# A place for the wait on a batch's rows, and an order of their own for the last two batches, in the attention layers of a graph network

## The reference, cut to what matters

```python
def _gat_layer(h, W, al, ar, src, dst, residual):
    feat = (h @ W).reshape(N, 4, 64)
    el, er = jnp.sum(feat * al[None], -1), jnp.sum(feat * ar[None], -1)
    e = leaky_relu(el[src] + er[dst], 0.2)
    ex = jnp.exp(e - segment_max(e, dst)[dst])
    a = ex / segment_sum(ex, dst)[dst]
    out = segment_sum(a[:, :, None] * feat[src], dst)
    return relu(out + h if residual else out)   # the last of the three has no residual
```

## Time and profile before

| | |
|---|---|
| median of three runs | 9299.58 us |
| the profiled execution, own time | 9322.28 us |
| its span | 9320.3 us |
| mean granted TensorE clock | 0.713 |
| the three attention layers | 3505 to 4936, 4937 to 6370, 6371 to about 7800 us |
| batches in a layer | 52 |

### The profile page before, as it was taken

How to read it: one execution, slowest core, us unless ns; L and a number is a source line. 1 busy time by engine, 2 the same in 40 slices (tenths; PEclk the granted TensorE clock), 3 DMA queues, 4 the chain that set the end, 5 groups by cost and what they waited for, 6 DMA issues and landing times. The chain is left out here.

```text
span 9320.3 us, 119336 instructions
## 1 busy us (share of the span) xinstructions
PE 4964.3 (53%) x16882; PEld 3061.1 (33%) x16882; DVE 4504.5 (48%) x11795; ACT 2930.1 (31%) x11603; POOL 4540.5 (49%) x4821
## 2 busy tenths in 40 slices
PE   9755555634444363566664655554656555444444
PEld 4333333423223242333332333332333332222222
DVE  4133333423333264666665666665666665333334
ACT  3200000000000034666663666663666663000000
POOL 0235555445545425555555555554555554554443
PEclk9866676767666686777776777776777777666667
DMA  6422222222222214333333343333333332222221
GB/s 194 141 66 81 82 80 82 73 67 78 72 67 73 64 59 131 107 108 106 107 106 87 106 109 104 107 111 107 109 107 108 105 107 72 77 77 73 77 74 58
DMA packets 449022, 866.69 MB, mean 93 GB/s; under 512 B 123533, under 2 KB 275494, under 8 KB 448266
## 3 DMA queue, kind: packets, MB, share of 16 engines
q0 software_dynamic: 227728, 627.56, 24.3%
q1 hardware_dynamic: 169632, 190.18, 6.3%
q10 hardware_dynamic: 50906, 41.33, 1.4%
HBM read 756.54 MB, written 102.11 MB: 92 GB/s over the span
## 5 line engine op out<-in xcount | busy, mean ns | idle before, releaser
L675 POOL DMA_INDIRECT rows_a<-table,rows_src x2460 | 2338.3, 951 | 1924.0 <-PE ps L2094 993.1
L878 PE MATMUL ps<-rows_a,hot_a 128*128 x4992 | 1812.8, 505 | 1840.2 <-DMA rows_a<-table 769.5
L2031 ACT ACTIVATE rows_a<-rows_a,ex_a 128x64 f32<-128x64 f32 x9600 | 2358.4, 337 | 167.5 <-issue 163.8
L799 DVE TENSOR_TENSOR agg<-agg,ps 128x256 f32 (+1 forms) x2496 | 1045.7, 419 | 2628.2 <-PE ps L878 1519.1
L2094 PE MATMUL ps<-rows_a,hot_a 128*128 128x260 f32 x4920 | 1972.3, 524 | 328.9 <-issue 185.8
L739 POOL DMA_INDIRECT rows_a<-table,rows_tile_a x1454 | 1377.2, 947 | 1443.8 <-PE ps L878 877.6
L878 PEld LDWEIGHTS ps<-rows_a,hot_a 128*128 128x128 f32 x4992 | 1133.1, 249 | 2434.4 <-issue 1781.1
L1943 DVE TENSOR_TENSOR agg<-agg,ps 128x260 f32 x2496 | 1044.1, 418 | 755.5 <-PE ps L2094 370.9
L2094 PEld LDWEIGHTS ps<-rows_a,hot_a 128*128 128x128 f32 x4920 | 1058.5, 248 | 663.5 <-issue 493.8
L739 POOL DMA_INDIRECT rows_a<-table,row x757 | 722.5, 954 | 713.2 <-PE ps L878 448.4
L2184 ACT ACTIVATE root_a<-mv_a,eps 128x1 f32<-128x1 f32 x49 | 14.4, 295 | 1495.4 <-issue 1075.2
(11 more groups left out here) (355 smaller groups left out, 4159.6 us busy)
## 6 DMA issues: line engine op xcount, KB each, us to landing
rows_a<-table SPq DMA_DIRECT2D x5760, 1.0 KB
dstt_a<-dloc_dram SPq DMA_DIRECT2D x156, 512.0 KB
own_a<-table SPq DMA_DIRECT2D x4608, 1.0 KB
rows_a<-table ACTq DMA_DIRECT2D x3840, 1.0 KB
table<-ob SPq DMA_DIRECT2D x48, 1024.0 KB, 4.4
rows_a<-table,rows_src POOLq DMA_INDIRECT x2460
rows_a<-table,rows_tile_a POOLq DMA_INDIRECT x1454
table<-ob_n SPq DMA_DIRECT2D x98, 130.0 KB
```

Source lines behind the costliest of these rows:

```text
L675: nc.gpsimd.indirect_dma_start(out=rows[:, n % ring, 0:width], out_offset=None, in_=table, in_offset=bass.IndirectOffsetOnAxis(ap=index[:, ...
L799: nc.vector.tensor_tensor(acc, acc, ps[n % banks][:, 0:width], ALU.add).then_inc(added, 1)
L878: nc.tensor.matmul(ps[n % banks][:, 0:width], hot[:, m % nbuf, j, :], mine[n % 4], start=True, stop=True).then_inc(step_done, 1)
L2031: ins = nc.scalar.mul(a, a, ex[:, k % GV, s, h:h + 1])
```

## The change: what it does

1. In the steady loop, which now runs over k = 0 to KG - 3, `logit_parts(n + 1)` moves from between the tenth and the eleventh accumulation to behind the sixteenth, just ahead of the next iteration's `rescale`.
2. Batch KG - 2 = 50 gets an order of its own on VectorE and TensorE. `logit_parts(51)` stands in it behind the third accumulation. The links (scans, transposes, logits) of batch 51 come after accumulations 3, 4, 5 and 6 instead of 0, 2, 5 and 9; `one_hots(50, 1)` stands ahead of the first accumulation. TensorE does the sixteen matmuls of `er_of_edges(51)` in one go behind product 0.
3. Batch 51 has a short loop of its own.

```diff
-                for k in range(KG):
-                    n = k + 1 if k + 1 < KG else None
+                for k in range(KG - 2):
+                    n = k + 1
...
                     accumulate(k, 10, acc[2])
-                    if n and n + 1 < KG:
-                        logit_parts(n + 1)
                     accumulate(k, 11, acc[3])
...
                     for j in range(13, 16):
                         accumulate(k, j, acc[j - 12])
-                        if j == 14 and n:
+                        if j == 14:
                             first = accs(n, 0)
+                    if n + 1 < KG - 1:
+                        logit_parts(n + 1)
                     acc = first
+
+                k, n = KG - 2, KG - 1
+                rescale(k, acc[0])
+                one_hots(k, 1)
+                accumulate(k, 0, acc[0])
+                accumulate(k, 1, acc[1])
+                accumulate(k, 2, acc[2])
+                logit_parts(n)
+                accumulate(k, 3, acc[3])
+                acc = accs(k, 1)
+                within_rows(n)
+                accumulate(k, 4, acc[0])
+                across_rows(n)
+                accumulate(k, 5, acc[1])
+                tops(n)
+                accumulate(k, 6, acc[2])
+                edge_sums(n)
+                logits(n)
+                accumulate(k, 7, acc[3])
+                one_hots(n, 0)
+                growth(n)
+                for q in (2, 3):
+                    acc = accs(k, q)
+                    for j in range(4):
+                        accumulate(k, q * 4 + j, acc[j])
+                rescale(n, accs(n, 0)[0])
+                for q in range(4):
+                    acc = accs(n, q)
+                    for j in range(4):
+                        accumulate(n, q * 4 + j, acc[j])
+                        if q * 4 + j == 1:
+                            one_hots(n, 1)
                 after.dve_last(dve)
```

TensorE's loop keeps its order for k up to KG - 3 and ends with:

```diff
+                k, n = KG - 2, KG - 1
+                sums(k, 0, 1)
+                for q in range(4):
+                    er_of_edges(n, q, er_rows(n, q))
+                sums(k, 1, 4)
+                turn(n)
+                sums(k, 4, 5)
+                turn_ends(n)
+                sums(k, 5, 6)
+                turn_carries(n)
+                sums(k, 6, 7)
+                turn_tops(n)
+                sums(k, 7, 12)
+                factor(n)
+                sums(k, 12, 16)
+                sums(n, 0, 16)
                 after.pe_last(pe)
```

More of the change, by code:

```diff
@@ L1964, in _ @@
                 acc = accs(0, 0)
-                for k in range(KG):
-                    n = k + 1 if k + 1 < KG else None
+                for k in range(KG - 2):
+                    n = k + 1
                     rescale(k, acc[0])
                     accumulate(k, 0, acc[0])
-                    if n:
-                        within_rows(n)
+                    within_rows(n)
                     accumulate(k, 1, acc[1])
@@ L1973, in _ @@
                     accumulate(k, 2, acc[2])
-                    if n:
-                        across_rows(n)
+                    across_rows(n)
                     accumulate(k, 3, acc[3])
@@ L1979, in _ @@
                     accumulate(k, 5, acc[1])
-                    if n:
-                        tops(n)
+                    tops(n)
                     accumulate(k, 6, acc[2])
                     accumulate(k, 7, acc[3])
-                    if n:
-                        one_hots(n, 0)
+                    one_hots(n, 0)
                     acc = accs(k, 2)
@@ L1988, in _ @@
                     accumulate(k, 9, acc[1])
-                    if n:
-                        edge_sums(n)
-                        logits(n)
+                    edge_sums(n)
+                    logits(n)
                     accumulate(k, 10, acc[2])
-                    if n and n + 1 < KG:
-                        logit_parts(n + 1)
                     accumulate(k, 11, acc[3])
-                    if n:
-                        growth(n)
+                    growth(n)
                     acc = accs(k, 3)
                     accumulate(k, 12, acc[0])
-                    if n and n + 1 < KG:
-                        edge_hots(n + 1)
+                    edge_hots(n + 1)
                     for j in range(13, 16):
                         accumulate(k, j, acc[j - 12])
-                        if j == 14 and n:
+                        if j == 14:
                             first = accs(n, 0)
+                    if n + 1 < KG - 1:
+                        logit_parts(n + 1)
                     acc = first
+                k, n = KG - 2, KG - 1
[7 more added lines that the diff above has]
+                acc = accs(k, 1)
+                within_rows(n)
+                accumulate(k, 4, acc[0])
+                across_rows(n)
+                accumulate(k, 5, acc[1])
+                tops(n)
+                accumulate(k, 6, acc[2])
+                edge_sums(n)
+                logits(n)
+                accumulate(k, 7, acc[3])
+                one_hots(n, 0)
+                growth(n)
+                for q in (2, 3):
[9 more added lines that the diff above has]
+                            one_hots(n, 1)
                 after.dve_last(dve)
@@ L2109, in _ @@
                 factor(0)
-                for k in range(KG):
-                    n = k + 1 if k + 1 < KG else None
+                for k in range(KG - 2):
+                    n = k + 1
                     sums(k, 0, 1)
-                    if n:
-                        turn(n)
-                        er_of_edges(n, 0, er_rows(n, 0))
+                    turn(n)
+                    er_of_edges(n, 0, er_rows(n, 0))
                     sums(k, 1, 3)
-                    if n:
-                        turn_ends(n)
+                    turn_ends(n)
                     sums(k, 3, 4)
-                    if n:
-                        er_of_edges(n, 1, er_rows(n, 1))
+                    er_of_edges(n, 1, er_rows(n, 1))
                     sums(k, 4, 6)
-                    if n:
-                        turn_carries(n)
+                    turn_carries(n)
                     sums(k, 6, 7)
-                    if n:
-                        er_of_edges(n, 2, er_rows(n, 2))
+                    er_of_edges(n, 2, er_rows(n, 2))
                     sums(k, 7, 8)
-                    if n:
-                        er_of_edges(n, 3, er_rows(n, 3))
+                    er_of_edges(n, 3, er_rows(n, 3))
                     sums(k, 8, 9)
-                    if n:
-                        turn_tops(n)
+                    turn_tops(n)
                     sums(k, 9, 15)
-                    if n:
-                        factor(n)
+                    factor(n)
                     sums(k, 15, 16)
+                k, n = KG - 2, KG - 1
[3 more added lines that the diff above has]
+                sums(k, 1, 4)
+                turn(n)
+                sums(k, 4, 5)
+                turn_ends(n)
+                sums(k, 5, 6)
+                turn_carries(n)
+                sums(k, 6, 7)
+                turn_tops(n)
+                sums(k, 7, 12)
+                factor(n)
+                sums(k, 12, 16)
+                sums(n, 0, 16)
                 after.pe_last(pe)
```

## The result

The changed kernel takes 9326.24 us in the median of 10 runs (9305.83 to 9345.64), the kernel before 9298.19 us beside it (10 runs, 9276.23 to 9326.65). The ratio is 1.0030, with a 95% interval from 1.0020 to 1.0041. The forecast was 9289 us.

A forecast was written before the change was run, and what follows sets the result against it. SP's issuing of single-row requests, slowed by GpSimd's gathers, was taken as the bound. A shift gaining 11.3 us less 0.9 for the last two batches gave 10.4 us off 9299.6: 9289 us, range 9262 to 9312.

The forecast's parts named there:

- the gain is a shift: Steady loop: landings stay 106.9 us apart; restart 5.45 us earlier less 1.7 for two gathers, 3.75 us a layer.
- the same 63 gathers in each four batches: Steady loop: SP's stream of fetches and loads, beside 63 gathers per four batches, is the same before and after.
- that short wait: VectorE's wait after a layer's second own step, where the shift taken at the first was said to be made up again.
- Two prices: SP's requests beside GpSimd's gathers: 0.9 us of SP per us of gather, and 1.5 us per gather in the burst.
- three signs: Wrong if waits' sum falls over 60 us, cycle leaves 106 to 108, or layer changes by other than 2 to 6.
- SP's issuing paces the layer: Attention layers: SP needs 106.9 us per four batches, VectorE about 95.5, so VectorE's wait at L1856 is slack.
- The waits stay: At L1856, VectorE's wait for own rows should remain, 33 times, about 380 to 410 us in all.
- the third rival: At L1856 the wait shrinks each time: 33 x 5.7 = 188 us off, 9111 us; chance 0.05.
- The two gathers more before the first landing: GpSimd puts two more gathers ahead of SP's last requests, making the landing 1.7 us later.
- The rule of the Trainium skill: DMA issue time is usually small beside transfers; by it own rows are late through transfers, each wait could shrink.
- The last two batches: Iterations 50 and 51: +0.3 us a layer, +0.9 us for three; bounds 5.9 us less to 2 more a layer.
- The second rival: SP's requests: gathers closer together slow every cycle, 1.35 us a cycle over 33 cycles, 45 us less 10: 9334 us; chance 0.10.

The follow-up runs named there:

- the last experiment: Kernel before, with `logit_parts(n + 1)` at the iteration's end only for k of 44 and more: 9213.41 us beside 9223.59, ratio 0.9988.
- the order alone: Kernel before with only the new order of the last two batches, the wait in its old place: 9228.03 us beside 9223.09, ratio 1.0005.
- the move alone: Kernel before with only `logit_parts(n + 1)` moved to the iteration's end, old order of the last two batches: 9238.1 us beside 9223.09, ratio 1.0018.
- the early: Kernel before with `logit_parts(n + 1)` at the iteration's end only for k under 8: 9328.9 us beside 9312.03, ratio 1.0015.
- the late move: Kernel before with `logit_parts(n + 1)` at the iteration's end only for k of 8 and more: 9330.79 us beside 9312.03, ratio 1.0019.
- group 4: One chip's kernels: before with gathers held four more products, 9220.96 us; before with a memset ahead of each gather, 9096.07; changed kernel with memsets, 9128.19.

## Why the prediction was wrong

**The step that failed** is "If landings keep their distance of 106.9 us, the restarts behind them keep it too", with "the gain is a shift, taken at a layer's first own wait (and again made up after the second, where the wait was short) and kept to the end". The gain was worked out as 3.75 us a layer, and it is 9.6 us of loss. SP's stream of requests is the same in number, as the prediction said, but not in time:

- The first two distances together are 6.2 us longer. In the kernel before VectorE's second wait was 1.5, 0.8 and 0.0 us, the cycle up to it took 96.2 us (the kernels without own rows have 94.9) with 58 to 60 gathers in it, and the next 110.0 us with 66 to 68. With the change all three waits are real (12.2, 6.9 and 7.3 us), and both cycles have 63 gathers. So "the same 63 gathers in each four batches" was wrong for just these two. Over all chips, and without memsets, the first distance is 105.1 to 106.4 us on average in the four kernels in which the early waits are moved, and 96.2 to 100.7 in the five in which they aren't; with the second distance they make 210.1 to 212.4 against 203.6 to 207.4. Single layers scatter: of the last experiment's, two need 202.8 and 199.3 us for the two distances and the third 211.0, all with the early waits in the old place. The prediction had that short wait in its rows and booked it as a place where the shift is made up. It was a cycle that the shift spoiled.
- Each later distance is 0.67 us longer: +0.9 from the order alone to the move alone (the pair whose profiled executions lie too far apart), and +0.8 from the early to the late move. The price per gather isn't one number.

Two prices in its working were loose, by less than 1 us of the whole each: 8.3 us more for 8.3 of gathering is 1.0 per us, and not 0.9, and 59.9/41 = 1.5 us a gather also counts the time of the 32 requests themselves.

Of the three signs that the prediction gave of being wrong only one came: a layer's length changed by 9.6 us, outside 2 to 6. The waits' sum fell by 15 us and the later distances, at 107.3 us, stayed inside 106 to 108, so these two would have passed a forecast that was wrong.

**Right steps.** SP's issuing paces the layer and VectorE's wait is slack: shown by taking the own rows away. The waits stay (391.3 us; 380 to 410 was said), though 36 of them, and the third rival, each wait shrinking, is dead. The restart after a landing went from 5.7 to 0.1 us. The two gathers more before the first landing are in the trace (80 instead of 78), and the landing came 1.6 us later, where 1.7 had been worked out; the three layers show -2.4, +5.3 and +2.0, so that this agreement is partly luck. And where the shift can be kept, behind the last landing, it is kept: -10.2 us in the last experiment, alone. The rule of the Trainium skill that was weighed there ("DMA: Bandwidth & Descriptors", section "Issuing engines are not separate DMA queues": the time in which a sequencer initiates DMAs is usually small beside the transfers) is not borne out here: one-row requests of 1 KB, 77.7 us for 128 beside gathers, cost this kernel 391 us, and the last rows were there 1.0 to 1.2 us after the last request wherever VectorE waited 8 us or more for them in the kernel before. With the rows fetched by GpSimd the same bytes moved, and the wait was gone.

**The last two batches** were said to cost 0.3 us a layer. VectorE's busy time in iterations 50 and 51 after, answering to the earlier trace rows:

```profile
4904.63:4923.04 18.41, 15.04 (x47) 0.65 0.03 9
4923.04:4935.01 11.97, 9.11 (x24) 1.00 0.03 11
```

They take 30.4 us, 1.1 more, where the prediction allowed up to 30. Half of it is bookkeeping that the prediction missed: `logit_parts(51)` was in iteration 49 and is now in 50, 0.27 us with 0.34 us of idle time before it. The rest, from all engines' timeline in iteration 50 of the changed kernel (the second and third line answer to the earlier trace rows):

```profile
4908.41 0.27 DVE L1850 TENSOR_TENSOR el_a<-rows_a,mneg 128x64 f32<-128x64 f32 x1 [0.34 <-issue]
...
4916.82 0.38 ACT L1441 ACTIVATE xt_n<-ps 128x256 f32<-128x256 f32 x1 [11.54 <-PE ps L1417]
4917.10 0.25 ACT L2041 ACTIVATE ex_a<-z_a 128x68 f32<-128x68 f32 x1
4917.43 0.64 DVE L1925 TENSOR_SCALAR am_a<-ex_a,cont 1x4 f32<-1x4 f32 x1
```

ScalarE's copy is the gate of the exponential, as was said, directly ahead of it; `growth`'s first instruction shows 0.64 us instead of 0.22, so its cover was a little short. Net of the moved call the time from the last landing to the layer's end is 0.4 us longer with both parts than with the move alone (122.4 and 122.0) and 0.8 us longer with the order alone than in the kernel before (127.5 and 126.7), on different chips. The step is a mis-sized term, of 1 or 2 us in the whole, and no part of the failure.

**The second rival** is the nearest to what happened: SP slower in every cycle. That gathers closer together do it is my reading of the table, with the memsets for it in part only. Its price, 1.3 us for a gather moved into a dense stretch, is the one in the table above, while the gathers that left the thin quarter gave back 0.44. It had taken 1.35 us a cycle, which would be 9334 us; the cycles show 0.67, and the loss at the second own step came on top. It was given 0.10 because the number of gathers in a cycle doesn't change. That is true of the nine later cycles and no argument, since SP's time for the same number differs. The note "it decides from 0.9 us a cycle" left out the first two cycles: with them 0.67 was enough.

**Open.** That the moved wait lengthens SP's cycles is shown; that it does so by denser gathers is argued from the table. Why a gather would cost SP's requests more when it follows another closely is not shown; the runs only show that the requests are faster with 0.13 us more between the gathers. The memsets also change what GpSimd does in that time, and no run parted the two. The distances and quarters come from one profiled execution of each kernel. Why the kernel before leaves the fast cycle after its second own step and never comes back was not tested. Its gathers (58 to 60 in that cycle, 66 to 68 in the next) go along with it, and the wait itself explains nothing, as it is short whenever SP's fetch was quick.

## What to carry to other kernels

A wait that a saturated queue leaves behind is slack, and a part of its length can't be cashed by moving it; what such a move does change is when the other engines run against that queue, and by this table that is to be priced by stretches, with the dense stretch's price for what comes in and the thin one's for what goes out. Here a gain that was taken once was kept only behind the last turn of the cycle. When a shared resource paces the loop, first try to take work off the pacing queue (4.3% here), then to spread what runs against it (1.6%), and only then to reorder the waits (0.3%, of the wrong sign).

## What the runs showed of the hardware

- SP's one-row requests of 1 KB took 10.28 us for 32 (0.32 us each) where no gather ran and 23.02 us (0.72 us each) beside 15, with SP waiting for nothing: the third line of the kernel before's stretches above is the dense part, and this is the empty one, GpSimd in the kernel before:

```profile
5268.08:5278.36 10.28, 0.00 (x0) 0.50 0.04 11
```

- A chain of indirect gathers on GpSimd with a 0.15 us memset before each, 1.38 us apart instead of 1.25, went with requests of another engine's queue that took 73.6 us for 128 instead of 77.3 (group 4 of the table), and made the kernel faster by 128 us, though GpSimd did more.
- One loop with the same requests took 96.2 us in the cycle up to a layer's second own step, with 58 to 60 gathers in it, 110.0 in the next, with 66 to 68, and 106.7 in the later ones, with 63 (the kernel before, means of three layers).
